# Batch 0 in another order: x in halves, k1's load first, layer 1 before the heads, and batch 1's FFN within batch 0's heads

## What is computed

```python
xn = layernorm(x)                                   # 16 x 512 x 256
q, k, v = xn @ wq, xn @ wk, xn @ wv                 # 8 heads of 128
q, k = rope(q), rope(k)
p = softmax(q @ k.T / 128 - 1e30 * (i < j))
attn = sum over heads of (p @ v) @ wo
h = s0 * (concat([xn, -xn]) @ sign(k0))             # 512 -> 1024
h = s1 * ((relu(h) * 2) @ sign(k1))                 # 1024 -> 1024
ffn = s2 * ((relu(h) * 2) @ sign(k2))               # 1024 -> 256
out = x + attn + ffn
```

## Time and profile before

| | |
|---|---|
| median of 3 runs | 1806.74 us (1805.23 to 1807.58) |
| span of the profiled execution | 1803.8 us |
| PE / DVE busy | 1758.1 us (97%) / 1442.7 us (80%) |
| ACT / POOL busy | 1092.3 us (61%) / 1044.7 us (58%) |
| chain that ended last | PE 92%, DVE 6%, POOL 1%, ACT 1% |
| x load, to landing | 512 KB, 4.0 us (median of 16) |
| k1 load, to landing | 1024 KB, 11.4 us |

### The profile page before, as it was taken

One profiled execution on the slowest core, in us unless ns is written; L12 is line 12 of the kernel. 1 busy time (PEld: TensorE's weight loads), 2 busy tenths in 40 slices (PEclk: granted clock), 3 DMA queues, 4 the chain that ended last, 5 costly groups with the idle time before them and its releaser, 6 DMA issues.

```text
span 1803.8 us, 30379 instructions
## 1 busy us (share of the span) xinstructions
PE 1758.1 (97%) x11272; PEld 1055.4 (59%) x11272; DVE 1442.7 (80%) x3271; ACT 1092.3 (61%) x2340; POOL 1044.7 (58%) x1067
## 2 busy tenths in 40 slices
PE   4889999999999999999999999999999999999999
PEld 2345656566565656656566665665656566565566
DVE  5999787887878788787887878878787887878865
ACT  4666565665656556566565756656566565665653
POOL 5475565655656556565555556546565665655552
PEclk8999999999999999999999999999999999999999
DMA  5143343434343334433434434344334333434433
GB/s 169 31 84 57 77 82 59 92 62 77 66 83 75 64 78 71 77 69 73 83 61 77 75 66 89 57 77 73 85 65 72 72 69 77 77 65 83 69 67 65
DMA packets 454805, 133.84 MB, mean 74 GB/s; under 512 B 434689, under 2 KB 453633, under 8 KB 454657
## 3 DMA queue, kind: packets, MB, share of 16 engines
q1 hardware_dynamic: 454656, 131.90, 38.2%
HBM read 14.94 MB, written 8.39 MB: 13 GB/s over the span
## 4 chain that ended last, share of the span: by engine, by line
PE 92%; DVE 6%; POOL 1%; ACT 1%; issue 0%; DMA 0%; DVEq 0%; POOLq 0%
PE bank L351 92%; DVE ph L542 1%; DVE p L507 1%; DVE qk L479 1%; DVE am L239 0%; DVE ta L463 0%; DVE h L393 0%; POOL w L309 0%; ACT p L521 0%; DVE v L396 0%; DMA xnat<-in_x 0%; DVE wo L266 0%; POOL ta L469 0%; DVE xp L233 0%; DVE bn L218 0%
## 5 line engine op out<-in xcount | busy, mean ns | idle before, releaser
L536 POOL TENSOR_SCALAR ph<-p,ri 128x512 f16<-128x512 f32 (+3 forms) x512 | 340.9, 666 | 311.7 <-DVE rk L528 277.0
L467 POOL TENSOR_TENSOR tb<-tb,sin 128x512 f32<-128x512 f32 x256 | 328.6, 1284 | 304.9 <-ACT tb L457 301.8
L351 PE MATMUL bank<-h,w 128*128 128x512 f16 x2048 | 463.7, 380 | 0.0
L469 POOL TENSOR_TENSOR ta<-ta,tb 128x512 f32<-128x512 f32 x256 | 343.9, 1343 | 55.8 <-DVE ta L463 38.6
L521 ACT ACTIVATE p<-p,nm,sc 128x512 f32<-128x512 f32 (+3 forms) x512 | 327.4, 641 | 36.8 <-DVE nm L515 36.7
L456 ACT ACTIVATE tb<-bank 64x512 f32<-64x512 f32 x256 | 152.2, 594 | 295.9 <-PE bank L351 285.0
L351 PEld LDWEIGHTS bank<-h,w 128*128 128x128 f16 x2048 | 199.2, 98 | 218.2 <-ACT w L312 0.8
L542 DVE SCALAR_TENSOR_TENSOR ph<-p,rk,ph 128x512 f16<-128x512 f32 (+3 forms) x512 | 304.9, 636 | 4.3 <-POOL ph L536 4.3
L475 ACT ACTIVATE qk<-ta 128x512 f16<-128x512 f32 x256 | 160.1, 625 | 180.7 <-POOL ta L469 180.7
L463 DVE TENSOR_TENSOR ta<-bank,cos 128x512 f32<-128x512 f32 x256 | 175.6, 686 | 99.5 <-ACT tb L457 99.3
L351 PE MATMUL bank<-qk 128*128 128x512 f16 (+3 forms) x1536 | 231.1, 300 | 21.9 <-DVE qk L479 21.9
(11 more groups left out here) (76 smaller groups left out, 1711.3 us busy)
## 6 DMA issues: line engine op xcount, KB each, us to landing
xnat<-in_x SPq DMA_DIRECT2D x16, 512.0 KB, 4.0
out<-xnat SPq DMA_DIRECT2D x32, 256.0 KB, 2.4
pt<-ph SPq DMA_TRANSPOSE x256, 4.3
v<-in_wq SPq DMA_DIRECT2D x1, 1024.0 KB, 6.9
v<-in_wk SPq DMA_DIRECT2D x1, 1024.0 KB, 8.9
o<-in_k SPq DMA_DIRECT2D x1, 1024.0 KB, 11.4
h<-in_wv SPq DMA_DIRECT2D x1, 1024.0 KB, 10.0
pt<-in_wo SPq DMA_DIRECT2D x1, 1024.0 KB, 12.6
```

What stands on the lines that cost most here:

```text
L351: self.todo.append(lambda e: e.matmul(self.ps[:, cols[0]:cols[1]], lhsT, rhs, start=start, stop=stop))
L467: a = pool.put(lambda e: e.tensor_tensor(tb, tb, SIN[:], ALU.mult))
L469: done["rot", n] = pool.put(lambda e: e.tensor_tensor(ta, ta, tb, ALU.add))
L536: done["P_hi", g, i] = pool.put(lambda e: e.tensor_scalar(part(r, i, HI), v, RI[:, g % 4, i:i + 1], 4096.0, ALU.mult, ALU.mult))
```

## The change

The loads: x of batch 0 comes in two DMAs, so the statistics of its first half can start on `x_first`. k1 is loaded right after k0, k2 ahead of wv, and wo last of all, when both subtractions of k0 are done, since it now lands in O[4:8], where k0 was. wv lands in PH; the pads of PH are written after wv's split, and the first two heads' high parts wait for it. K0F is gone: DVE subtracts k0's bytes (`subtract_k0`, from 8-bit to float16) and ACT multiplies by the sign (`sign_k0`) in place of one ACT and one POOL conversion and a DVE subtraction for each half.

The order: all of layer 0, and `layer1(0, 0)` and `layer1(0, 1)`, come ahead of the loop. The rest of batch 0's layer 1 is in passes -2 (n = 2, 3), -1 (4, 5, 6) and 0 (7), its layer 2 in passes 1 and 2. Batch 1's layer 0 is in passes 2 and 3 and its layer 1 in passes 4 to 11, one fill in each. `normal(1)` moves from pass 3 to pass -1, wo's split from pass -1 to pass 2, wv's from pass -1 to pass -2. From batch 2 on all passes are as before.

```diff
@@ -140,14 +141,13 @@
         stage = {
             "q": V[:, 0].rearrange("p a b -> p (a b)").bitcast(F32),
             "k": V[:, 1].rearrange("p a b -> p (a b)").bitcast(F32),
-            "o": PT[:].rearrange("p r a b -> p (r a b)")[:, 0:4096].bitcast(F32),
+            "v": PH[:].rearrange("p r n -> p (r n)")[:, 0:4096].bitcast(F32),
+            "o": O[:, 4:8].rearrange("p a b c -> p (a b c)").bitcast(F32),
         }
         stage3 = {n: v.rearrange("p (c n) -> p c n", c=1 if n == "o" else 2) for n, v in stage.items()}
-        stage3["v"] = H1[:, :, 4:8].rearrange("p c a b -> p c (a b)").bitcast(F32)
         K1S = O[:, 0:4].rearrange("p a b c -> p (a b c)").bitcast(U8)
         K0S = O[:, 4:6].rearrange("p a b c -> p (a b c)").bitcast(U8)
-        K0F = TA[:].rearrange("p a b -> p (a b)")[:, 0:1024].bitcast(F16)
-        K2S = O[:, 6:7].rearrange("p a b c -> p (a b c)").bitcast(U8)
+        K2S = O[:, 8:9].rearrange("p a b c -> p (a b c)").bitcast(U8)
 
         pe, dve, act, pool = (Queue(sem("s_" + n)) for n in ("pe", "dve", "act", "pool"))
         sp = Queue(None)
...
-        x_load(0)
+        first = x[0].rearrange("(t p) m -> p t m", p=128)
+        done["x_first"] = sp.dma(lambda e: e.dma_start(X[:, 0, 0:2], first[:, 0:2]), s_first, 16)
+        done["x", 0] = sp.dma(lambda e: e.dma_start(X[:, 0, 2:4], first[:, 2:4]), s_x[0], 16)
         done["s3"] = sp.dma(lambda e: e.dma_start(S3[:], s3), s_s3, 16)
         k_load(0, K0S, k0)
+        k_load(1, K1S, k1)
         w_load("q", wq.rearrange("(c p) h d -> p c (h d)", p=128))
         w_load("k", wk.rearrange("(c p) h d -> p c (h d)", p=128))
-        k_load(1, K1S, k1)
         done["cos"] = sp.dma(lambda e: e.dma_start(COS[:], cosT), s_cos, 16)
         done["sin"] = sp.dma(lambda e: e.dma_start(SIN[:], sinT), s_sin, 16)
+        k_load(2, K2S, k2)
+
         w_load("v", wv.rearrange("(c p) h d -> p c (h d)", p=128))
-        w_load("o", wo.rearrange("h d m -> d h m"))
-        k_load(2, K2S, k2)
         x_load(1)
+
+        def last_load():
+
+            sp.wait(done["k0_diff", 0], done["k0_diff", 1])
+            w_load("o", wo.rearrange("h d m -> d h m"))
 
...
                     xn(b)[:, t, :], X[:, r, t, :], MV[:, r, t, 0:1], RS[:, r, t:t + 1], ALU.subtract, ALU.mult))
 
 
@@ -271,12 +288,15 @@
             dve.wait(done["s3"])
             a = dve.put(lambda e: e.tensor_scalar(SG[:, 0:3], S3[:], 0.0, None, ALU.is_ge))
             dve.wait(a)
-            a = dve.put(lambda e: e.tensor_scalar(SG[:, 0:3], SG[:, 0:3], 2.0, -1.0, ALU.mult, ALU.add))
-            dve.wait(a)
+            done["signs"] = dve.put(lambda e: e.tensor_scalar(SG[:, 0:3], SG[:, 0:3], 2.0, -1.0, ALU.mult, ALU.add))
...
             dve.put(lambda e: e.tensor_scalar(SG[:, 4:5], SG[:, 1:2], -2.0 ** -9, None, ALU.mult))
             a = dve.put(lambda e: e.tensor_tensor(SC[:, 2:4], S3[:, 0:2], SG[:, 0:2], ALU.mult))
-            done["signs"] = a
+            done["k1_signs"] = a
             dve.wait(a)
             a = dve.put(lambda e: e.tensor_scalar(SC[:, 4:5], SC[:, 2:3], SC[:, 3:4], 64.0, ALU.mult, ALU.mult))
             dve.wait(a)
@@ -285,24 +305,21 @@
         def halves(v, half):
             return v.rearrange("p (c n) -> p c n", c=2)[:, :, half * 512:half * 512 + 512]
 
-        def convert_k0(half):
-
-            act.wait(done["k_in", 0], done["signs"])
-            done["k0_low", half] = act.put(lambda e: e.activation(
-                halves(K0F, half), halves(K0S[:, 2048:4096], half), ACT.Copy, scale=SG[:, 0:1]))
-            pool.wait(done["k_in", 0], done["signs"])
-            done["k0_high", half] = pool.put(lambda e: e.tensor_scalar(
-                W0[:, :, half * 512:half * 512 + 512], halves(K0S[:, 0:2048], half), SG[:, 0:1], 0.0,
-                ALU.mult, ALU.add))
-
         def subtract_k0(half):
 
-            dve.wait(done["k0_high", half], done["k0_low", half])
+            dve.wait(done["k_in", 0])
+            done["k0_diff", half] = dve.put(lambda e: e.tensor_tensor(
+                W0[:, :, half * 512:half * 512 + 512], halves(K0S[:, 0:2048], half), halves(K0S[:, 2048:4096], half),
+                ALU.subtract))
+
+        def sign_k0(half):
+
+            act.wait(done["k0_diff", half], done["signs"])
             w0 = W0[:, :, half * 512:half * 512 + 512]
-            done["W0", half] = dve.put(lambda e: e.tensor_tensor(w0, w0, halves(K0F, half), ALU.subtract))
...
+            fs = [Fill(("T", c)) for c in range(2)]
+            for t in range(4):
+                pe.wait(done["xn", 0, t])
+                for c, f in enumerate(fs):
                     f.turn((t * 128, t * 128 + 128), xn(0)[:, t, c * 128:c * 128 + 128])
-                f.end([("xT", 0, c)])
+                    if t < 3:
+                        f.begin()
+                    else:
+                        f.end([("xT", 0, c)])
+            for c, f in enumerate(fs):
                 split(f, XT[:, 0, HI, :, c, :], XT[:, 0, LO, :, c, :], ("xT_hi", c), ("xT", 0, c))
 
...
                 pool.wait(need(("inv_k", g)))
+                if g < 2:
+                    pool.wait(done["W", "v", 0], done["W", "v", 1])
...
 
+        def staged(s):
+
+            if s < 4:
+                return [("W1", k) for k in range(8)]
+            return [("W", "o", p) for p in range(2)] if s < 8 else ["W2"]
+
         def values(g):
...
                 for n in range(8):
-                    add_filler(z - 2 + n // 4, n % 4, lambda n=n, b=b: layer0(b, n))
+                    add_filler((z if b > 1 else 4) - 2 + n // 4, n % 4, lambda n=n, b=b: layer0(b, n))
                 for t, (slot, order) in enumerate(((-2, 4), (0, 0), (0, 2), (0, 3))):
                     add_filler(z + slot, order, lambda b=b, t=t: v_proj(b, 0, t))
             else:
-                for n in (6, 7):
-                    add_filler(-2, n, lambda n=n: layer0(0, n))
                 for t in range(4):
                     add_filler(0, 4, lambda t=t: v_proj(0, 0, t))
             for n, slot in enumerate((0, 1, 2, 3, 4, 4, 5, 5)):
                 if last:
                     slot = (0, 1, 2, 3, 4, 5, 5, 6)[n]
                 elif b == 0:
-                    slot = (-1, -1, 0, 0, 1, 2, 4, 5)[n]
+                    if n < FIRST:
+                        continue
+                    slot = (-2, -2, -2, -2, -1, -1, -1, 0)[n]
+                elif b == 1:
+                    slot = (-4, -3, -2, -1, 0, 1, 2, 3)[n]
                 add_filler(z + slot, 1 if n < 5 else 3, lambda b=b, n=n: layer1(b, n))
             for t, (slot, order) in enumerate(((3, 0), (3, 2), (3, 3), (4, 2))):
                 add_filler(z + slot, order, lambda b=b, t=t: v_proj(b, 1, t))
             for k in range(2):
-                add_filler(z + (7 if last else 6 + k), 5, lambda b=b, k=k: layer2(b, k))
+                add_filler(z + (7 if last else 6 + k if b else 1 + k), 5, lambda b=b, k=k: layer2(b, k))
                 if not last:
...
-        for half in range(2):
-            convert_k0(half)
+        subtract_k0(0)
+        sign_k0(0)
         norm_apply(0)
+        subtract_k0(1)
+        last_load()
+        ffn_scales()
         first_T()
-        largest(0, "q")
         while later:
             later.pop(0)[1]()
-        for half in range(2):
-            subtract_k0(half)
+        sign_k0(1)
+        pool.wait(done["xn", 0])
+        convert_k1(pool, 0, 5)
+        convert_k1(act, 5, 8)
+        largest(0, "q")
         largest(1, "k")
-        for n in range(6):
+        for n in range(8):
             layer0(0, n)
+            run_due()
+        layer1(0, 0)
+        run_due()
         powers(0, 2.0 ** -10)
         split_w("q", 0, 0, 4)
         split_w("k", 1, 0, 4)
         a = dve.put(lambda e: e.tensor_scalar(SC[:, 0:1], P2[:, 0:1], P2[:, 1:2], 2.0 ** -7, ALU.mult, ALU.mult))
         dve.wait(a)
         done["scale"] = dve.put(lambda e: e.tensor_scalar(SC[:, 1:2], SC[:, 0:1], -1.0, None, ALU.mult))
-        convert_k1(pool, 3, 8)
+        layer1(0, 1)
+        run_due()
...
+            if g == -2:
+                split_w("q", 0, 1, 4)
+                split_w("k", 1, 1, 4)
+                convert_k2()
+                largest(2, "v")
+                largest(3, "o")
+                powers(2, 2.0 ** -30)
+                for p in range(2):
+                    split_w("v", 2, p, 2)
+                pads()
+            if g == -1:
+                for p in (2, 3):
+                    split_w("q", 0, p, 4)
+                    split_w("k", 1, p, 4)
+            if g == 2:
+                for p in range(2):
+                    split_w("o", 3, p, 2)
+                done["attn_scale"] = dve.put(lambda e: e.tensor_scalar(SC[:, 6:7], P2[:, 2:3], P2[:, 3:4], None,
+                                                                       ALU.mult))
             for job in third[0]:
                 job()
                 run_due()
             if 0 <= g + 1 < G:
                 scores(g + 1)
```

(5 more changed lines are left out.)

58 lines of the change are left out of this document (24 added, 34 removed).

## The result

| | before | after |
|---|---|---|
| median | 1806.58 us (1805.23 to 1807.58, 4 runs) | 1819.24 us (1818.64 to 1822.18, 4 runs) |
| ratio to before | | 1.0074 (95% interval 1.0059 to 1.0088) |
| span of the profiled execution | 1803.8 us | 1820.1 us |
| PE busy | 1758.1 us | 1763.6 us |

The change made the kernel **0.74% slower**; the prediction, 1798 us in a range of 1786 to 1809, was wrong in sign and size. The profiled executions differ by 16.3 us, the medians by 12.7: the changed kernel's profiled execution is its slowest of four (1822.18 us), and the span of before, 1803.8, is as short as any of that kernel's in the later runs (1803.8 to 1806.9). Of the 16.3 us, PE stands still 10.8 us longer and is busy 5.5 us longer with the same 11272 matmuls.

A forecast was written before the change was run, and what follows sets the result against it. PE, busy 1758.1 of 1803.8 us, was the bound, with DVE behind its stops. Stops of 17.2 + 10.3 + 5.0 + 1 = 33.5 against 42.4 gave 1794.9; 2.9 more for the median made 1798, range 1786 to 1809.

The forecast's parts named there:

- Layer 0 at 12.8: Kernel start: layer 0 begins at 12.8 us, 2.4 sooner than before, range 11.5 to 15.
- Fills until 44.7: Start: PE has layer-1 fills and q and k of heads 0 and 1 to do until 44.7 us.
- scores(0) at 51.1: Head 0's scores can start at 51.1 us, after PE stands still for 6.4 us.
- rival 2: Start: no measurable change, 1803 to 1810, as the chain to scores(0) takes 7 us more; chance 0.20.
- scores(2) at 77.8: PE reaches head 2's scores at 77.8 us, against 78.70 before; PE's stops to here 17.2 us.
- Passes 1 to 7, 10.3 us of stops: PE waits 10.3 us in these passes, with DVE at 10.1 us a head against PE's own work.
- 10.1 us of DVE a head: DVE's cost of one head while DVE is behind, from the stretch scores(2) to scores(8) before the change.
- Rival 1: Heads cost less, 1790 us; sign: passes 4 to 7 without stops; chance 0.25 with all below 1793.
- Passes 8 to 15, 5.0 us: Stops of 5.0 us where there were none: 4.4 between scores(12) and scores(15), 0.6 in pass 14.
- 38.0 us of DVE: From scores(12) to scores(15): three heads at 10.1, norm(2) 4.7, five evictions 3.0, against 26.8 us of PE.
- Rival 3: Slower, about 1831: ten PE-poor heads cost 13.4 us each, adding 33 us; chance 0.13 with other losses.
- The clock: Half speed (1.2 GHz) once, around PE's stop ahead of scores(0), as before: no gain or loss.

The follow-up runs named there:

- ffn1_back: Changed kernel with batch 1's layer 1 back in passes 8 to 13, two fills each in 12 and 13: 1828.03 us.
- early_parts: Changed kernel with high and low parts of q and k of heads 14 and 15 written into ACT's and DVE's queues earlier: 1818.34 us.
- norm2_small: Changed kernel with batch 2's layer norm on only 64 of 256 columns, leaving its result incomplete: 1816.82 us.
- pads_late: Changed kernel with POOL's clearing of the pads moved to pass -1, after head 0's rotation: 1814.51 us.
- both_late: Changed kernel with the pads cleared after head 0's rotation and k2's conversion moved to pass 0: 1812.52 us.
- k2_late: Changed kernel with k2's conversion on POOL moved from between the two all-reduces to pass 0: 1820.38 us.
- one_reduce: Changed kernel with one all-reduce for all four weights, both moves of both_late, and the third layer-1 fill ahead of the loop: 1807.54 us.
- best_start: Changed kernel with one_reduce's edits, splits behind head 0's rotation, batch 1's layer 1 in passes 4 to 8 and 11 to 13: 1798.35 us.
- best_head0: best_start with head 0's high and low parts of q and k also written early (delays 14 and 18): 1801.17 us.

## Why the prediction was wrong, point by point

The profiled execution was forecast at 1794.9 and took 1820.1, 25.2 more; the median was forecast at 1798 and came out at 1819.24, 21.2 more. The points below go by the profiled execution, which is a slow one of its kernel, so about 3 us of them are not the kernel's. A time above 1810.3 had been given 0.13.

- **Layer 0 at 12.8**: 13.36. The subtraction of k0 took 1.23 (put at 1.1), the applies 1.38 (1.5); what came last was ACT's second multiplication by the sign. Right.
- **Fills until 44.7**: the last layer-1 fill ran from 40.95 to 44.57. Right to 0.2.
- **scores(0) at 51.1: 61.75.** This is the first step that failed, by 10.7 us (8.7 to 10.3 in the four other runs with this start). "All-reduce and scales to 39.6" became 42.6, since POOL could begin its second all-reduce only at 41.44, 3.3 after the maxima. "POOL is held until wv's low parts at 43.2 and clears the pads (1.2), then four rotation steps" put the 7.06 us before the rotation at nothing. The rest of this chain, 1.2 for the pads, 5.5 for the rotation (5.2), 1.5 for the parts (1.5), fits. That was rival 2's place and its test (later than 56); at 7 us it had been put too low, and at 0.20 too unlikely.
- **scores(2) at 77.8**: 91.31, that is 2.9 more than the first failure explains; two waits behind DVE (2.22 and 1.63) in pass 0 weren't in the sum, and PE's own work there was 1.0 less than put.
- **Passes 1 to 7, 10.3 us of stops**: 8.3, and 2.5 of one layer-2 fill at half speed (6.18 at 114.05). The sum came out right by luck, not by 10.1 us of DVE a head: the low parts of the probabilities took 852 ns on average from scores(2) to scores(8), not 1007, and DVE was busy only 79.16 of 88.80 us to scores(9). Rival 1's sign, no stops in passes 4 to 7, didn't come either: 1.34, 0.48 and 0.78 us.
- **Passes 8 to 15, 5.0 us: 17.5** (0.73, 7.46, 4.00 and 5.3 of slow matmuls). The second failure, 12.5 us. The sum made DVE the bound with 38.0 us of work from scores(12) to scores(15). DVE was in truth busy 32.7 of the 41.3 us, less than forecast, and PE waited longer. The step that failed is the term "38.0 us of DVE" as the bound: a pass that PE could do in 7 us takes over 14, because its head's parts wait in queues whose order is set by counts of PE's work (ffn1_back, early_parts), with DVE's load (norm2_small) and the norm's chain close beneath. Rival 3 had a price near it, 13.4 a head, from the earlier trace rows, but as DVE's cost and for ten heads. DVE was busy 16.58 of 17.09 us in that row and 8.35 of 14.11 in ffn1_back's first window, so that the numbers are alike is chance.
- **The clock, "I expect the same once, so no gain or loss"**: it was lost again after the stops at 250 and 264.6 and among the short ones around 110. PE's busy time is 5.5 of the 16.3 us, a term that I didn't have.

These add up to 10.7 + 2.9 + 0.5 + 12.5 = 26.6; 1.4 less came elsewhere, the 1 us of small stops among it. Against the kernel before: the start won some 2 us of waiting on transposes, the stop ahead of scores(0) took 5.3 more (17.18 against 11.90), passes 13 and 14 took 11.5 that had not been there, and all other waits together fell by 4.1: 10.8 us in sum.

That the pause ahead of the rotation sets scores(0) was shown by moving it (pads_late, both_late); the part of layer 1 by three edits. What stays open is how the stops at 250 and 264.6 share out among order, load and norm: each edit moved the next one up.

## What to carry to other kernels

Read the bracket of a row, not only its duration: an idle time that ends in "issue" is a cost with no name, and it moves with the instruction. Put POOL's all-reduces next to each other, or merge them, and keep them off a chain that PE waits for. Before an engine is called the bound of a pass, look at its busy time in a pass where PE waits: if it is 8.4 of 14 us, look at the order of the queues first. The next limit may lie right beneath: early_parts took 8.5 us of stops away and met a new one of 5.1.

## What the runs showed of the hardware

- POOL's change from arithmetic to PARTITION_ALL_REDUCE took 5.92 and 7.24 us in the changed kernel and 8.80 in pads_late, the change back 7.86 and 7.06 in the changed kernel, 7.09 in pads_late, 7.44 in k2_late, 7.00 in both_late and 7.03 in one_reduce (whose row names ACT's copy, done 0.5 us before); there was none between two all-reduces, and none before a MEMSET. The Trainium skill, GPSIMD Engine Reference, section 2.1, gives about 6 us for the first call of a freshly loaded routine on this engine, without an instruction in the profile. By these rows it is 5.9 to 8.8 us, it comes back at every change, and the way back to arithmetic costs it as well. What POOL does in this time no run shows.
- Half speed (granted 0.50, that is 1.2 GHz) followed stops of 17.18, 7.46 and 4.00 us, and once a group of stops of 1.5 to 2.1. A stop of 2.52 was followed by it in best_start; one of 2.75 in best_head0 and one of 4.00 in pads_late were not. The length of a stop alone doesn't tell.
